# Three fp32r passes over halves for the compressed value product, P turned into two separate banks, and one rotary product moved to GpSimd

## Time and profile before

| | |
|---|---|
| median of 3 runs | 2539.03 us (2535.17 to 2539.18) |
| the profiled execution | 2538.65 us |
| its span in the profile | 2536.9 us |
| matmul instructions | 15288 |

### The profile page before, as it was taken

One profiled execution on the slowest core, in us unless ns is written; L12 is line 12 of the kernel. 1 busy time (PEld: TensorE's weight loads), 2 busy tenths in 40 slices (PEclk: granted clock), 3 DMA queues, 4 the chain that ended last, 5 costly groups with the idle time before them and its releaser, 6 DMA issues. The chain is left out here.

```text
span 2536.9 us, 54996 instructions
## 1 busy us (share of the span) xinstructions
PE 2503.8 (99%) x15288; PEld 2216.7 (87%) x15320; DVE 1978.9 (78%) x6309; ACT 1657.2 (65%) x4674; POOL 1565.8 (62%) x2766
## 2 busy tenths in 40 slices
PE   6999999999999999999999999999999999999999
PEld 5888888888888888888888888888888888888888
DVE  6788888888777787778777777778877777777776
ACT  4666666666666666667666666666675666666665
POOL 5787776776676555555556555555556656555654
PEclk8999999999999999999999999999999999999999
DMA  3432233323341221212333212212134122122101
GB/s 110 163 113 92 76 105 117 121 91 116 125 133 43 88 88 59 88 57 74 134 110 100 80 51 88 88 59 88 61 130 153 58 69 84 34 80 80 66 24 51
DMA packets 170596, 224.94 MB, mean 89 GB/s; under 512 B 18098, under 2 KB 89268, under 8 KB 170292
## 3 DMA queue, kind: packets, MB, share of 16 engines
q1 hardware_dynamic: 169716, 221.16, 26.4%
q10 hardware_dynamic: 576, 0.26, 0.1%
HBM read 158.44 MB, written 62.91 MB: 87 GB/s over the span
## 5 line engine op out<-in xcount | busy, mean ns | idle before, releaser
L1435 POOL TENSOR_TENSOR t<-raw,tB 128x128 f32<-128x128 f32 x512 | 227.1, 465 | 614.2 <-DVE raw L1040 614.0
L864 ACT ACTIVATE ch<-bVC,blT 128x128 fp32r<-128x128 f32 x512 | 160.4, 364 | 509.2 <-PE bVC L624 509.0
L1389 POOL TENSOR_TENSOR r<-ss,mh 128x4 f32<-128x4 f32 x256 | 291.3, 1138 | 264.8 <-DVE ss L1057 264.8
L550 PE MATMUL bQK<-wh,xh 128*128 128x512 f32 x1024 | 427.4, 417 | 0.8 <-DVE raw L1040 0.8
L551 PE MATMUL bQK<-wl,xh 128*128 128x512 f32 x1024 | 404.5, 395 | 0.0
L552 PE MATMUL bQK<-wh,xl 128*128 128x512 f32 x1024 | 403.1, 394 | 0.0
L1085 DVE CUSTOM_DVE_ANT_0 P<-bS,cst 128x256 f32<-128x256 f32 (+1 forms) x512 | 203.6, 398 | 151.6 <-PE bS L598 150.9
L566 PE MATMUL bVC<-wh,xh 128*128 128x256 f32 x1024 | 309.9, 303 | 0.0
L831 ACT ACTIVATE P<-P,nm,r 128x256 f32<-128x256 f32 (+1 forms) x512 | 295.2, 583 | 0.0
L568 PE MATMUL bVC<-wh,xl 128*128 128x256 f32 x1024 | 288.8, 282 | 0.0
L567 PE MATMUL bVC<-wl,xh 128*128 128x256 f32 x1024 | 288.7, 282 | 0.0
(11 more groups left out here) (157 smaller groups left out, 6963.1 us busy)
## 6 DMA issues: line engine op xcount, KB each, us to landing
wh<-kept SPq DMA_DIRECT2D x144, 256.0 KB, 4.0
wl<-kept SPq DMA_DIRECT2D x144, 256.0 KB, 4.6
kept<-wh SPq DMA_DIRECT2D x48, 256.0 KB, 3.2
kept<-wl SPq DMA_DIRECT2D x48, 256.0 KB, 3.5
woh<-kepto SPq DMA_DIRECT2D x48, 256.0 KB, 3.3
wol<-kepto SPq DMA_DIRECT2D x48, 256.0 KB, 3.9
ini<-in_hidden_states SPq DMA_DIRECT2D x24, 256.0 KB, 4.3
xs<-xsh SPq DMA_DIRECT2D x24, 256.0 KB, 2.6
```

Of the source, the lines that this page charges most:

```text
L550: e.matmul(bQK[:, :], a, b, start=kt == 0, stop=False)
L1389: e.tensor_tensor(r4[:, u % 4], ss[:, u % 4], mh[:, 0:4], ALU.pow).then_inc(S["r4"], 1)
```

## The change

1. The product of cv with the compressed P is done from halves. ScalarE makes the high half of P (hi_p) and of cv; VectorE makes the low halves (lo_p, lo_cv). values issues three fp32r matmuls of 256 columns for each block of 128 compressed keys instead of one plain fp32 one, and waits for pl and lo_p instead of p.
2. turn_p turns the local blocks of both heads into bP[0] and the compressed ones into bP[1]. put_p becomes put_l (one copy of both heads' local blocks, as plain fp32) and hi_p (one copy of both heads' compressed blocks, to fp32r).
3. The rotary product rope_a goes from VectorE to GpSimd, behind rope_b and ahead of rope_rest.
4. a8 and b8 shrink from nine tiles to four each. SyncE stores the casts of the first eight tiles to HBM (park_eights, in the tile's hi slot) and loads them two slots ahead of their use (fetch_eights). cast_x of tiles 4 to 7 waits for the store of the tile four before; the first cast of W2 waits for the stores of tiles 3 and 7.

```diff
+        pt = sb("pt", [128, 2, 256])
+        pch = sb("pch", [128, 2, 2, 128], F32R)
+        pcl = sb("pcl", [128, 2, 2, 128], F32R)
+        cvh = sb("cvh", [128, 2, 2, 128], F32R)
+        cvl = sb("cvl", [128, 2, 2, 128], F32R)
+        a8 = sb("a8", [128, 4, 512], F8)
+        b8 = sb("b8", [128, 4, 512], F8)
...
+            def park_eights(t):
+                e.wait_ge(S["b8"], t + 1)
+                for n, w in enumerate((a8, b8)):
+                    e.dma_start(eights[t, n], w[:, t % 4, :]).then_inc(S["d_e%d" % (t % 4)], 16)
+            def fetch_eights(t):
+                if t < 3:
+                    e.wait_ge(S["d_e%d" % t], 64)
+                else:
+                    e.wait_ge(S["qd"], KT + ffn_pos(t - 3) + 1)
+                for n, w in enumerate((a8, b8)):
+                    e.dma_start(w[:, t % 3, :], eights[t, n]).then_inc(S["d_8%d" % (t % 3)], 16)
...
             for s in range(FIRST, LAST):
+                if tile_at(s, "hi") is not None and tile_at(s, "hi") < 8:
+                    park_eights(tile_at(s, "hi"))
...
-            def turn_p(u, h):
-                a = 2 * u + h
-                e.wait_ge(S["norm"], a + 1)
-                if a >= 2:
-                    e.wait_ge(S["p"], a - 1)
-                for n, k in enumerate(pblocks(u)):
-                    last = e.transpose(bP[h][:, n * 128:(n + 1) * 128], P[:, u % 2, h, k * 128:(k + 1) * 128], ident)
-                last.then_inc(S["pt"], 1)
+            def turn_p(u):
+                nb = u % 8 // 4 + 1
+                for h in range(2):
+                    e.wait_ge(S["norm"], 2 * u + h + 1)
+                    if h == 0 and u >= 1:
+                        e.wait_ge(S["pl"], u)
+                    for n in range(nloc(u) // 128):
+                        last = e.transpose(bP[0][:, (2 * h + n) * 128:(2 * h + n + 1) * 128],
+                                           P[:, u % 2, h, n * 128:(n + 1) * 128], ident)
+                    if h == 1:
+                        last.then_inc(S["ptl"], 1)
+                    if h == 0 and u >= 1:
+                        e.wait_ge(S["lo_p"], u)
+                    for n in range(nb):
+                        last = e.transpose(bP[1][:, (2 * n + h) * 128:(2 * n + h + 1) * 128],
+                                           P[:, u % 2, h, 256 + n * 128:384 + n * 128], ident)
+                last.then_inc(S["ptc"], 1)
...
             def values(u, h):
                 if h == 0:
-                    e.wait_ge(S["p"], 2 * u + 2)
+                    e.wait_ge(S["pl"], u + 1)
+                    e.wait_ge(S["lo_p"], u + 1)
...
-                        c = slice((len(ts_) + n) * 128, (len(ts_) + n + 1) * 128)
-                        e.matmul(bVC[:, 256:512], cv[:, b % 2, n, :], pt[:, :, c], start=n == 0, stop=False)
+                        ph, pl_ = pair(pch[:, n]), pair(pcl[:, n])
+                        e.matmul(bVC[:, 256:512], cvh[:, b % 2, n, :], ph, start=n == 0, stop=False)
+                        e.matmul(bVC[:, 256:512], cvh[:, b % 2, n, :], pl_, start=False, stop=False)
+                        e.matmul(bVC[:, 256:512], cvl[:, b % 2, n, :], ph, start=False, stop=False)
...
-            def put_p(u, h):
-                n = len(pblocks(u)) * 128
-                e.wait_ge(S["pt"], 2 * u + h + 1)
-                if u >= 1:
-                    e.wait_ge(S["c"], 2 * (u - 1) + h + 1)
-                e.activation(pt[:, h, 0:n], bP[h][:, 0:n], ACT.Copy).then_inc(S["p"], 1)
+            def put_l(u):
+                n = nloc(u)
+                e.wait_ge(S["ptl"], u + 1)
+                if u >= 1:
+                    e.wait_ge(S["c"], 2 * (u - 1) + 2)
+                e.activation(pt[:, :, 0:n], bP[0][:, :].rearrange("p (h c) -> p h c", h=2)[:, :, 0:n],
+                             ACT.Copy).then_inc(S["pl"], 1)
+            def hi_p(u):
+                nb = u % 8 // 4 + 1
+                e.wait_ge(S["ptc"], u + 1)
+                if u >= 1:
+                    e.wait_ge(S["c"], 2 * (u - 1) + 2)
+                e.activation(flat(pch[:, 0:nb]), bP[1][:, 0:nb * 256], ACT.Copy).then_inc(S["hi_p"], 1)
...
             def cast_x(t):
+                if 4 <= t < 8:
+                    e.wait_ge(S["d_e%d" % (t % 4)], 32)
...
-            def rope_a(u):
-                ...
-                e.tensor_tensor(t1[:, :, :, :], raw[:, u % 2, :, :, 0:64],
-                                tA[:, :, u % 8, :].unsqueeze(1).broadcast_to([128, 2, 2, 64]), ALU.mult).then_inc(S["t1"], 1)
...
+            def lo_p(u):
+                n = (u % 8 // 4 + 1) * 256
+                e.wait_ge(S["hi_p"], u + 1)
+                nb = u % 8 // 4 + 1
+                e.tensor_tensor(flat(pcl[:, 0:nb]), bP[1][:, 0:n], f32(flat(pch[:, 0:nb])),
+                                ALU.subtract).then_inc(S["lo_p"], 1)
+            def lo_cv(k):
+                b = k // 2
+                e.wait_ge(S["css"], k + 1)
+                e.tensor_tensor(cvl[:, b % 2, k % 2, :], bY[:, 128:256], f32(cvh[:, b % 2, k % 2, :]),
+                                ALU.subtract).then_inc(S["lo_cv"], 1)
...
                 if u5 is not None:
                     add_out(u5)
+                if u3 is not None:
+                    lo_p(u3)
...
             def rope_b(u):
                 last.then_inc(S["t2"], 1)
+                e.tensor_tensor(t1[:, :, :, :], raw[:, u % 2, :, :, 0:64],
+                                tA[:, :, u % 8, :].unsqueeze(1).broadcast_to([128, 2, 2, 64]), ALU.mult).then_inc(S["t1"], 1)
```

More of the change, by code:

```diff
@@ L276, in slot8 @@
         def slot8(t):
-            return min(t, NT)
+            return t % 4 if t < 8 else 3
         def bc(ap, n):
@@ L515, in run_sync @@
                     store_whole(t)
+                if ffn_at(s, -2) is not None and ffn_at(s, -2) < 8:
+                    fetch_eights(ffn_at(s, -2))
                 if ffn_at(s, 1) is not None and ffn_at(s, 1) < 8:
@@ L758, in run_tensor @@
                 if u3 is not None:
[L759 to L760 removed]
+                    turn_p(u3)
                 if u1 is not None:
@@ L769, in run_tensor @@
                 values(n - 3, h)
-            for h in range(2):
-                turn_p(n - 2, h)
+            turn_p(n - 2)
             for h in range(2):
@@ L776, in run_tensor @@
             proj_v(n)
-            for h in range(2):
-                turn_p(n - 1, h)
+            turn_p(n - 1)
             for h in range(2):
@@ L784, in run_tensor @@
                 values(n - 1, h)
-            for h in range(2):
-                turn_p(n, h)
+            turn_p(n)
             for h in range(2):
@@ L1013, in run_scalar @@
                 exp_l(n - 1, h)
-            for h in range(2):
-                put_p(n - 2, h)
+            put_l(n - 2)
+            hi_p(n - 2)
             put_v(n)
@@ L1023, in run_scalar @@
             hi_c(n - 2)
-            for h in range(2):
-                put_p(n - 1, h)
+            put_l(n - 1)
+            hi_p(n - 1)
             hi_c(n - 1)
-            for h in range(2):
-                put_p(n, h)
+            put_l(n)
+            hi_p(n)
             hi_c(n)
@@ L1286, in run_vector @@
                     lo_x(tile_at(s, "lo"))
+                if block_at(s, "put") is not None:
+                    lo_cv(block_at(s, "put"))
                 if block_at(s, "rope") is not None:
@@ L1365, in run_vector @@
                     lo_c(n - 3)
+                else:
+                    lo_p(n - 2)
                 strike(u, 0)
```

50 lines of the change are left out of this document (23 added, 27 removed), and 2 rows, old and new, of the table SIGNALS.

## The result

| | before | after |
|---|---|---|
| median of 4 runs | 2539.11 us (2535.17 to 2539.40) | 2514.76 us (2514.18 to 2517.16) |
| profiled execution | 2538.65 us | 2515.21 us |
| ratio after / before | | 0.9909, interval 0.9892 to 0.9927 |

The change takes 24.4 us off by the medians and 23.4 us between the two profiled executions. The forecast was 2515.6 us and a sum of 23.4 us. That a sum comes out does not show that its terms do, so each is looked at by itself.

What follows compares the result with a forecast made beforehand. The prediction took TensorE's stream, priced by the spacing of matmul starts, to bound the kernel. Its terms, -29.2 + 4.5 + 1.3 = -23.4 us, gave 2515.6 us against the median of 2539.03, range 2508 to 2529.

Steps and rivals of the forecast that it cites:

- The product: Compressed value product on TensorE: three fp32r passes take 0.354 us a block instead of 0.43; 384 blocks save 29.2 us.
- Transposes and ScalarE's copies: Transposes of P keep number and shape, ScalarE's copies change only in size; 0 on TensorE's stream.
- The low half in ordinary slots: VectorE's new subtraction before the product fits into 1.83 us of room; 0 us, with VectorE some 30 us busier.
- The five early slots: Units 2, 4, 7, 9 and 12: VectorE is late after extra work and TensorE waits; +4.5 us, bounds 0 and 10.
- The rotary product: Moved to GpSimd: 0.85 us each, fitting into 1.27 us of idle time there, GpSimd to about 70%; cost 0.
- DMA and start: Storing and reloading the fp8 tiles, and the prologue: nothing comes late; 0 us, bounds 0 and 3.
- The tail: Last units, without room: the subtraction follows ScalarE's copies and delays two products by 0.8 and 0.5 us; +1.3 us.
- (1): Rival: saving right, but VectorE is late more often, held by GpSimd's shifted rows; 2530 us, 2522 to 2534; chance 0.17.
- (2): Rival: low half late in every slot, the addition being held by GpSimd's scaling and power; 2593 us; chance 0.06.
- (3): Rival: the product's third weight load is not hidden, 0.57 us a block, +54 us; 2599 us; chance 0.02.
- (4): Rival: waits and a shifted start cancel the saving; within 5 us of 2539; chance 0.05.

Runs made afterwards that it cites:

- e1_plain: The changed kernel with the three passes of the compressed product replaced by one plain fp32 matmul of the two high halves; 2542.81 us.
- e5_six: The changed kernel with each of the three 256-column passes cut into two of 128, six passes a block; 2630.55 us.
- e6_low_thrice: The changed kernel with VectorE's subtraction for the low half of P done three times over; 2584.48 us.
- e2_rotary_back: The changed kernel with the rotary product back on VectorE in its old place; 2524.21 us.
- e8_load_early: The changed kernel with the load of the next x tile at the head of SyncE's slot, ahead of weight chunks and stores; 2512.11 us.
- e9_load_early_low_first: The changed kernel with the x tile's load at the head of SyncE's slot and the low-half subtraction ahead of the accumulation into acc; 2511.98 us.

## Why the prediction was right, step by step

**The sum.** It is right to 0.1 us partly by luck. By the slots, the product was worth 0.4 us more than forecast, the early waits were 1.8 us less, the tail 0.9 us more and the start 1.3 us more, and these four cancel. What carries the forecast is the one large term.

**What bounds the kernel.** Right: TensorE's stream. The sign of printed busy time (+124 us for the product) was the wrong one, that of the spacings the right one.

**The product**, -29.2 us: 0.077 us a block instead of 0.076, 29.6 us by the late slots and 28.0 by e1_plain. The passes lie 0.119 us apart, forecast 0.118. By the 262 cycles of the Trainium skill (page TensorE: Matmul & The Clock Gate, section Back-to-back issue gap), which stand there for a matmul by itself, it would have been an estimated 40 us; the measured spacing stays above it. Nothing was lost for the third load, in any slot, and e5_six suggests that the margin is small: 0.119 us at 256 columns, 0.112 at half of them.

**Transposes and ScalarE's copies**, 0: copies of 588 and 599 ns for 512 columns, 365 and 372 for 256; ScalarE is 15 us less busy than before. Right.

**The low half in ordinary slots**, 0: right, 681 and 414 ns against 692 and 420. That VectorE would be some 30 us busier was wrong: it is 19 us less busy. The 1.8 us of room are there in the slot shown; by e6_low_thrice 0.6 us is left in the tightest of the late slots.

**The five early slots**, +4.5 us: the sign and the stretch right, 2.7 us by slots, 2.0 us as waits of L654 ahead of 200 us where 3 to 6 were forecast. The units are not the ones that were priced: the largest, unit 4 with 1.6 us, did not wait at all, unit 9 waited 0.21 us instead of 1.3, units 7 and 12 0.58 and 0.92 us, and unit 1, not named, 0.31. In e2_rotary_back, with the rotary product on VectorE, units 4, 9 and 12 did wait 1.79, 1.66 and 2.02 us. So over-counted was how late VectorE is: the sum gave it back the 0.46 us of the moved product, and not the 0.75 us of additions no longer held by GpSimd's quantisation product.

**The rotary product**, 735 ns instead of 0.85 us, hidden, GpSimd at 69% against 70: right as a cost of 0. But it is not merely free. The prediction did not ask what the change would be without it: 9.5 us worse. And it reasoned that the addition could start 0.46 us earlier, not that this takes it out of GpSimd's quantisation product.

**DMA and start**, 0: right for the parking. The +1.3 us at the start are at the edge of what executions differ by, and open. Not seen at all was that VectorE waits for an x tile, 1.75 and 1.04 us in the kernel before and 1.27 and 1.28 in the changed one; it does not change the sum, but a slow landing there can hide what another edit is worth.

**The tail**, +1.3 us: 2.2. The two waits forecast were there, 1.06 and 0.33 us of TensorE; missed was a third, at L637: turn_p of unit 254 waits for the subtraction of unit 253, queued behind the masks of unit 255. The changed kernel's row of 1.3 us is that.

**The rivals.** (1) VectorE late more often: only as the mild form above. (2) The addition held by the scaling and the power: refuted, 446 ns on average and none over 0.9 us. By the Trainium skill's page SBUF — State Buffer, section SBUF: two separate sides, whichever starts first has the lock for the whole instruction. The trace agrees: the held additions all started second. The prediction counted the power's row against that page, but in the slot shown, as in all 213 where the two overlap in the changed kernel, the power starts inside the addition, so it is the addition that was first, and the power that could be held: its mean is 1.14 us there and 1.02 elsewhere. Whether a power that started first would hold the addition, no row shows. (3) The third load not hidden: refuted by spacing and by e1_plain. (4) Cancelled by the waits: the waits are 3.6 us by e1_plain, 6 by the slots with the start.

**The best version** is e8_load_early, 2512.11 us: the change with the x tile's load at the head of SyncE's slot, 2.6 us under the changed kernel and 26.6 under the kernel before run beside it. e9_load_early_low_first, 2511.98 us, is no different from it.

## What to carry to other kernels

Price a TensorE edit by the spacing of starts in a stretch that is already full, and never by printed durations: here they gave +124 us for what saved 29. When an instruction is moved between two engines, look not only at what it costs there but at what it pushes behind or ahead of what; where both counted, the order of two instructions on GpSimd gave VectorE more (0.75 us) than the 0.46 us moved. And before an edit worth 2 us is called worthless, compare the traces slot by slot: here one load that took 4.4 to 4.9 us instead of 3.5 to 3.9, and the lower clock behind the wait for it, hid a gain that was there in the other slots.

## What the runs showed of the hardware that was not expected

- VectorE's addition of two SBUF tiles, 0.41 us, lasts until 0.28 us after GpSimd's bf16 product of 128x512 if it starts inside it (1.16 and 1.17 us in the rows shown, 34 times in 256). In the changed kernel, where it starts ahead of the product, no addition lasts over 0.8 us (0.41 in the row shown), and a product that starts inside one lasts 1.21 to 1.35 us instead of 1.17.
- Not every instruction of GpSimd holds VectorE. L1206, one operation on 128x512 in fp32, kept its 0.54 us in the six tiles of the changed kernel in which it started inside a power on 128x4; inside a quantisation product it took 0.88 us (two tiles), and inside keep_8 (L1470) up to 1.07 us (14 tiles). One of the six:

```profile
367.13 1.02 POOL L1448 TENSOR_TENSOR r<-ss,mh 128x4 f32<-128x4 f32 x1
...
367.54 0.54 DVE L1206 TENSOR_SCALAR xt<-ini,st 128x512 f32<-128x512 f32 x1
```

- An fp32r matmul with a weight load of its own starts 0.112 us after the last with 128 columns and 0.119 with 256: half the columns save next to nothing.
- A wait of 2.16 us of TensorE in the tail, after 4 us of which it was busy for 3.23, was followed by a granted clock of 0.54 for some 3 us; one of 1.06 us at the same place was not. In slot 45 waits of 2.35 and 2.84 us were, and one of 2.18 us was not.
